# A Mamba2 mixer and feed-forward layer on one core: ACT's gaps moved ahead of the drains, one addition a step later, an earlier root in the last unit, and the prologue's stores issued by SP

## The reference

```
proj = x @ in_proj_w.T                      # 1024 tokens x 512 -> gate, hBC, dt
hBC  = silu(causal_conv4(hBC) + conv_b)     # -> hs (128 heads x 64), B, C (8 groups x 128)
dt   = clip(softplus(dt + dt_bias), 0, 100)
A_cum = cumsum(dt * -exp(A_log)) in chunks of 128 tokens
Y_diag = (C B^T * L) (hs * dt)              # L[l,s] = exp(A_cum[l] - A_cum[s]), s <= l
Y_off  = C . state . exp(A_cum)             # state carried from chunk to chunk
y = (Y_diag + Y_off + hs * D) * silu(gate)
out = rmsnorm_per_group(y) * norm_w @ out_proj_w.T
x = layernorm(x + out);  x = layernorm(x + x @ W.T + bias + lora(x))
```

## Time and profile before

| what | value |
|---|---|
| median of 3 runs | 1631.5 us (1628.75 to 1632.23) |
| the profiled execution | 1630.76 us, its span 1628.9 us |
| mean granted TensorE clock | 0.996 of full speed |
| busy: PE, DVE, ACT, POOL | 1585.0, 1356.4, 1222.4, 1234.6 us |
| DMA | 178.69 MB, mean 110 GB/s |

### The profile page before, as it was taken

One profiled execution on the slowest core, in us unless ns is written; L12 is line 12 of the kernel. 1 busy time (PEld: TensorE's weight loads), 2 busy tenths in 40 slices (PEclk: granted clock), 3 DMA queues, 4 the chain that ended last, 5 costly groups with the idle time before them and its releaser, 6 DMA issues. The chain is left out here.

```text
span 1628.9 us, 27350 instructions
## 1 busy us (share of the span) xinstructions
PE 1585.0 (97%) x9104; PEld 1300.6 (80%) x9104; DVE 1356.4 (83%) x1877; ACT 1222.4 (75%) x2363; POOL 1234.6 (76%) x1019
## 2 busy tenths in 40 slices
PE   8899999999999999999999999999999999999987
PEld 6778888878888788878888788887888788887764
DVE  6577898879979798797988889887997879888786
ACT  5878778777778877886887777887687877778742
POOL 4478778687796868778787878868779696877883
PEclk9999999999999999999999999999999999999999
DMA  3543325233242432433243332423324233343311
GB/s 114 199 166 98 120 79 156 82 111 108 91 151 79 121 98 98 128 97 121 86 119 122 93 121 83 155 79 114 110 85 159 72 121 97 98 138 92 130 53 46
DMA packets 87148, 178.69 MB, mean 110 GB/s; under 512 B 16480, under 2 KB 20576, under 8 KB 86624
## 3 DMA queue, kind: packets, MB, share of 16 engines
q1 hardware_dynamic: 83760, 175.72, 34.0%
q10 hardware_dynamic: 3248, 1.22, 0.3%
HBM read 172.17 MB, written 4.72 MB: 109 GB/s over the span
## 5 line engine op out<-in xcount | busy, mean ns | idle before, releaser
L505 PE MATMUL proj<-x_hi,w_hi 128*128 128x512 f32 x1160 | 462.2, 398 | 11.2 <-DVE x_lo L1274 6.9
L506 PE MATMUL proj<-x_lo,w_hi 128*128 128x512 f32 x1160 | 453.4, 391 | 0.0
L507 PE MATMUL proj<-x_hi,w_lo 128*128 128x512 f32 x1160 | 453.1, 391 | 0.0
L996 POOL TENSOR_TENSOR w_lo<-raw,w_hi 128x512 fp32r<-128x512 f32 x209 | 284.9, 1366 | 110.8 <-ACT w_hi L732 108.1
L1149 DVE SCALAR_TENSOR_TENSOR hs<-proj,uch,hs 128x511 f32<-128x511 f32 (+2 forms) x384 | 285.3, 744 | 58.6 <-ACT hs L759 53.8
L813 ACT ACTIVATE decay<-decay,tok 128x128 f32<-128x128 f32 x1024 | 312.4, 390 | 0.0
L505 PEld LDWEIGHTS proj<-x_hi,w_hi 128*128 128x128 f32 x1160 | 219.0, 189 | 56.5 <-issue 10.5
L1054 POOL TENSOR_TENSOR dh<-dh,eac 128x512 f32<-128x512 f32 x96 | 128.7, 1340 | 169.7 <-DVE eac L1209 169.7
L507 PEld LDWEIGHTS proj<-x_hi,w_lo 128*128 128x128 f32 x1160 | 218.7, 189 | 46.3
L506 PEld LDWEIGHTS proj<-x_lo,w_hi 128*128 128x128 f32 x1160 | 219.1, 189 | 41.9
L1178 DVE TENSOR_TENSOR decay<-decay,cb 128x1024 f32<-128x1024 f32 x128 | 200.2, 1564 | 54.4 <-ACT decay L831 52.0
(11 more groups left out here) (129 smaller groups left out, 3031.4 us busy)
## 6 DMA issues: line engine op xcount, KB each, us to landing
decay<-acum_d SPq DMA_DIRECT2D x128, 512.0 KB, 4.2
raw<-w_t SPq DMA_DIRECT2D x209, 256.0 KB, 2.9
eac<-eacum_d SPq DMA_DIRECT2D x192, 128.0 KB, 3.0
wo_raw<-wo_t SPq DMA_DIRECT2D x32, 256.0 KB, 4.2
c_new<-wo_t SPq DMA_DIRECT2D x32, 256.0 KB, 3.7
hs<-x_t SPq DMA_DIRECT2D x8, 256.0 KB, 5.8
acc<-x_tok SPq DMA_DIRECT2D x1, 2048.0 KB, 8.9
out<-acc SPq DMA_DIRECT2D x8, 256.0 KB, 2.0
```

The lines of the kernel that those rows point to most:

```text
L505: nc.tensor.matmul(dst[:], w_hi[:, ws, k, :], x_hi[:, k, cols], start=(k == 0), stop=False)
L506: nc.tensor.matmul(dst[:], w_hi[:, ws, k, :], x_lo[:, k, cols], start=False, stop=False)
L507: mm = nc.tensor.matmul(dst[:], w_lo[:, ws, k, :], x_hi[:, k, cols], start=False, stop=(k == KC - 1))
L996: nc.gpsimd.tensor_tensor(w_lo[:, s].rearrange("p a b -> p (a b)"), raw[:, s, :], w_hi[:, s].rearrange("p a b -> p (a b)").bitcast(F32), A ...
```

## The change

Nothing is computed differently; instructions change their place in an engine's order, and four stores their engine.

- ACT, loop: in all steps but (g,e,1) (there only (0,0,1) changes), the gaps come ahead of the drain of a one-batch tile, and between the two drains of a two-batch tile. `lookahead` stays behind the last drain, so it comes behind the gaps.
- VectorE: at e = 0 the `add_normed` of chunk 5 moves from step 5 to step 6, which then has two. In the last unit `scale_off` of step 2 comes sooner, and in step 7 `ln_begin(0, 5)` stands directly behind `add_normed`.
- GpSimd, last unit: `rstd_of(0, .)` moves to the next step, behind the state's decay; where a step has no tiles, `decay_hidden` goes ahead of `skip`; in step 7 the root `rs` goes ahead of the gate.
- Prologue: SP issues the four stores, waits for their inputs itself, and issues the first load of `eac` there instead of in the loop. ACT drains H0 to H2 sooner, and takes the first exponential after the first batch's Silus.

```diff
-            wait(q, dh_ready, step(g, e, c))
+            wait(q, dh_ready, 0 if step(g, e, c) == 1 else step(g, e, c))
@@ SP, prologue
+            sp.wait_ge(scanned, 2)
+            sp.dma_start(acum_d.rearrange("c h l -> h c l"), sc[2].rearrange("h (c l) -> h c l", c=CHUNKS)).then_inc(acum_stored, 16)
+            sp.wait_ge(act_pre, 7)
+            for h2 in range(2):
+                sp.dma_start(eacum_d[:, h2].rearrange("c a l -> a c l"),
+                             sc[3][h2:HEADS:2].rearrange("a (c l) -> a c l", c=CHUNKS)).then_inc(eacum_stored, 16)
+            sp.dma_start(elast_d, elc[:]).then_inc(eacum_stored, 16)
             sp.wait_ge(acum_stored, 16)
             load_decay(sp, 0, 0, 0)
...
             sp.wait_ge(eacum_stored, 48)
+            load_eac(sp, 0, 0, 1)
@@ ACT, loop
-                        if tiles:
+                        o2, e2, c2 = ahead(e, c, 2)
+                        o3, e3, c3 = ahead(e, c, 3)
+                        if c == 1 and (g, e) != (0, 0):
                             drain_proj(g, tiles[0])
                             lookahead(g, e, c, 0, last)
-                        if c == 1 and (g, e) != (0, 0):
                             wo_split_hi(g, e, (2, 3))
...
+                            gaps(g + o3, e3, c3)
+                        else:
+                            if tiles and len(tiles[0].batches) == 2:
+                                drain_proj(g, tiles[0], (0,))
+                            if c % 2 == 0:
+                                gaps(g, e, c + 1)
+                            elif not (last and o3):
                                 gaps(g + o3, e3, c3)
-                        else:
-                            gaps(g, e, c + 1)
+                            if tiles:
+                                drain_proj(g, tiles[0], (1,) if len(tiles[0].batches) == 2 else (0,))
+                                lookahead(g, e, c, 0, last)
@@ GpSimd, loop
+                        if last and e == 1 and c >= 3:
+                            rstd_of(0, c - 3)
...
                         if not tiles:
+                            if c == 7:
+                                lagged_rms(g, e, c)
                             gate_y(g, e, c)
-                            lagged_rms(g, e, c)
+                            if c < 7:
+                                lagged_rms(g, e, c)
                             if not (last and off):
+                                decay_hidden(g + off, ne, ncn)
                                 skip(g + off, ne, ncn)
-                                decay_hidden(g + off, ne, ncn)
-                        if last and e == 1 and c >= 2:
-                            rstd_of(0, c - 2)
@@ VectorE, loop
-                        elif e == 0 and c >= 5 and not (g == 0):
+                        elif e == 0 and c >= 6 and not (g == 0):
+                            if c == 6:
+                                add_normed(g - 1, 5)
                             add_normed(g - 1, c)
...
+                        if ffn_step and c == 7:
+                            ln_begin(0, 5)
+                            lns = lns[1:]
```

More of the change, by code:

```diff
@@ L459, in body @@
                         o1, e1, c1 = ahead(e, c, 1)
-                        if c1 % CPB and not (last and o1):
+                        if c1 % CPB and not (last and o1) and (g, e, c) != (0, 0, 0):
                             load_eac(sp, g + o1, e1, c1)
@@ L875, in _ @@
             silus(None, [PROLOGUE[3]])
-            drain_proj(None, PROLOGUE[5], (0,))
+            drain_proj(None, PROLOGUE[5])
             act.wait_ge(scanned, 2)
-            act.dma_start(acum_d.rearrange("c h l -> h c l"), sc[2].rearrange("h (c l) -> h c l", c=CHUNKS)).then_inc(acum_stored, 16)
             v = sc[4].rearrange("p (c l) -> p c l", c=CHUNKS)
@@ L884, in _ @@
             ins.then_inc(act_pre, 1)
-            drain_proj(None, PROLOGUE[5], (1,))
+            drain_proj(None, PROLOGUE[6], (0,))
             nc.scalar.activation(elc[:], a[:, :, P - 1:P].rearrange("p c o -> p (c o)"), ACT.Exp).then_inc(act_pre, 1)
             nc.scalar.activation(sc[3], sc[2], ACT.Exp).then_inc(act_pre, 1)
[L888 to L893, removed]
+            drain_proj(None, PROLOGUE[6], (1,))
             lay_tokens(1, 0)
-            drain_proj(None, PROLOGUE[6], (1,))
-            drain_proj(None, PROLOGUE[7], (0,))
+            drain_proj(None, PROLOGUE[7])
             lay_tokens(2, 2)
@@ L904, in _ @@
             gaps(0, 0, 0)
-            drain_proj(None, PROLOGUE[7], (1,))
+            drain_proj(None, PROLOGUE[8], (0,))
+            silus(None, PROLOGUE[5:9], (0,))
+            drain_proj(None, PROLOGUE[8], (1,))
+            drain_proj(None, PROLOGUE[9])
             act.wait_ge(gap_ready, 1)
             exps(0)
[L908 to L912, removed]
             silus(None, PROLOGUE[5:9], (1,))
@@ L1120, in _ @@
             groups(body)
+            rstd_of(0, 5)
             inv_rms(G, 6)
@@ L1355, in body @@
                             add_normed(g, c - 2)
-                        elif e == 0 and c >= 5 and not (g == 0):
+                        elif e == 0 and c >= 6 and not (g == 0):
+                            if c == 6:
+                                add_normed(g - 1, 5)
                             add_normed(g - 1, c)
                         lns = [(w, c - (2, 5)[w]) for w in range(2) if ffn_step and c >= (2, 5)[w]]
-                        if ffn_step and c in (1, 4, 5, 6):
+                        if ffn_step and c in (1, 2, 4, 5, 6):
                             scale_off(g, e, c + 1)
+                        if ffn_step and c == 7:
+                            ln_begin(0, 5)
+                            lns = lns[1:]
                         for ln in lns:
@@ L1401, in body @@
                             low_gated(s)
-                        if ffn_step and c in (0, 2):
+                        if ffn_step and c == 0:
                             scale_off(g, e, c + 1)
```

## The result

The changed kernel takes 1637.45 us (median of 10 runs, 1633.1 to 1641.16) against 1629.67 for the kernel before in the same rounds: ratio 1.0044, 95% interval 1.0033 to 1.0056. It is 0.44% slower, some 7 us; the forecast was 1621 and the range ended at 1628. The profiled execution took 1635.34 us, its span 1633.5.

A forecast was written before the change was run, and what follows sets the result against it. TensorE, busy 1585.0 of 1628.9 us, was taken as the bound, leaving 44 us of idling to win. Terms -7.7 + 1.4 - 2.0 - 1.8 = -10.1 us gave 1621 us; 8-in-10 range 1612 to 1628.

The forecast's parts named there:

- (g,0,6), predicted 7 x 1.1 = 7.7 us: Step 6 at e = 0, groups 1 to 7: moving the addition removes TensorE's wait for `eac`, winning 7.7 us.
- Gaps ahead elsewhere, +0.2 a group, +1.4, ends -6.3 and +6.3: Other loop steps: gaps ahead of drains delay `w_hi` and GpSimd, costing 0.2 us a group, +1.4 in all.
- makes this wait 0.2 to 0.4 longer: TensorE's 0.94 us `p_out` wait at (g,0,1): GpSimd 1.3 us late lengthens it by 0.2 to 0.4 us.
- 1.07 us at (g,1,3): Step 3 at e = 1: time to spare between `xd_lo` ending and TensorE taking it, 1.07 us.
- I price it at nothing: VectorE's two additions in step 6 at e = 0 cost nothing; without cover, at most 1.7 us.
- Rival (A): Loop: the split behind the gaps makes `xd_lo` or `w_lo` TensorE's last wait; +16 us, 1647 us; chance 0.08.
- Prologue, predicted -2.0: Program start: earlier `eac` load and drains win 2.0 us; ends -4.5 and +1.0.
- the 1.6 us for the lower clock behind 48.17: Prologue: the late tile H2 ran at granted clock 0.63, costing 1.6 us that earlier drains would remove.
- Last unit, predicted -1.8: Program end: earlier root `rs` and reordering shorten TensorE's 2.66 us wait at 1602.24, winning 1.8 us; ends 0 and -3.5.
- its far end: Last unit's best case, -3.5 us: the wait gone and the lower clock behind it too.

The follow-up runs named there:

- e1: Kernel before with only the addition of chunk 5 moved from step (g,0,5) to (g,0,6): 1620.38 us, ratio 0.9946.
- e11: Changed kernel with ACT's split ahead of the gaps in one-batch steps and VectorE's third `wo_lo` ahead of the state addition at c = 1: 1606.84 us, ratio 0.9855.
- e5: Changed kernel with ACT's loop order as in the kernel before (gaps behind drains and split): 1614.21 us, ratio 0.9898.
- e3: Kernel before with the prologue's edits alone: 1628.18 us, ratio 0.9986.
- e2: Kernel before with ACT's loop order alone changed (gaps ahead of the drains): 1644.05 us, ratio 1.0082.
- e4: Kernel before with the last unit's VectorE and GpSimd edits alone: 1626.01 us, ratio 0.9978.
- e10: Changed kernel with VectorE's split of the last two output weights (`wo_lo` 2 and 3) moved later, behind `front`: 1639.38 us, ratio 1.0052 to the kernel before.
- e12: e11 with ACT's split (`lookahead`) ahead of the second drain in two-batch steps: 1603.90 us, ratio 0.9841 to the kernel before.

## Why the prediction was wrong

1. **(g,0,6), predicted 7 x 1.1 = 7.7 us: right in kind, too small.** The wait went in all seven groups; e1 measured 0.54%, 8.8 us, and the traces 1.45 us each, 10.2 in all. The idle entry was 1.22, but consecutive matmuls overlap by 0.24 in the records, and a wait costs that too: 1.22 + 0.24 = 1.46. The same sum holds for the new waits (0.73 + 0.24 against a lag of 1.00) and for e11 (0.47 + 0.24 against 0.75).
2. **"Gaps ahead elsewhere, +0.2 a group, +1.4, ends -6.3 and +6.3": the step that failed.** This term priced the late split. The step-by-step comparison of the changed kernel with e5 gives 1.21 + 1.00 + 0.55 - 0.23 = +2.5 a group, 17.7 us in seven groups, beyond the upper end. Two things were wrong in it.
   - At (g,0,1) I wrote that a GpSimd 1.3 us late "makes this wait 0.2 to 0.4 longer". `dh`, for which VectorE's `y` waits, ends at 469.66 + 1.74 = 471.40, 1.41 us later than before (469.99), while TensorE was 0.93 us ahead by that time: 2.34 us late against TensorE. VectorE's slack took up a part, and the wait grew by 1.21: 0.93 because the last two `wo_lo` start at the same time as before while TensorE is ahead, 0.28 because they take longer. The gate did get its 1 us back, 1.29 instead of 2.27, as predicted. But `w_lo` was 1.41 late and `dh` is still 1.41 late: the 1 us was paid by the instructions behind, above all by `rs` (1.54 instead of 0.54), which now runs beside VectorE's mix of 461.32 to 463.10, 2 us sooner than before, and by `dh` itself (1.74 instead of 1.29). That is what the Trainium skill's "SBUF — State Buffer", "Who interferes with whom", says, which I had weighed and set aside: the later one of the two blocks. Here the trace agrees with it.
   - (g,1,0) is not in the prediction. Its margin, 1.57 us, is in none of its rows; it took 1.07 us at (g,1,3) for the tightest and stood it in for the rest. That one was not touched: in two-batch steps ACT arrives early enough, as predicted, and no wait came. Nor did the prediction price the `proj` wait for `w_lo` at (g,1,1).
3. **"I price it at nothing": the addition in step 6.** True for VectorE, as e1 shows; but the gain itself has a price. TensorE arrives 1.45 us sooner at (g,1,0) and spends the margin on which the gaps edit rested. I priced the edits apart and added them. Rival (A) had the mechanism: its places (g,1,7) and (g,0,7), "about 1 each", are the ones that cost, those at (g,1,3) and (g,0,5) gave no wait; I gave it 0.08 because I let ACT's earlier arrival pay for it everywhere, and in the one-batch steps there is no idle time between drains from which it could.
4. **Prologue, predicted -2.0:** right, e3 -2.3 us (0.14%), with the wait near 75 (4.48 in e3, 4.09 in the changed kernel) and the clock behind it at 0.59 in both. One piece of its sum does not hold: the 1.6 us for the lower clock behind 48.17 is not a fixed cost. In e1, e2 and e4, whose prologue is that of before, the clock there was 1.00, and TensorE waited for the next tile instead (1.30 us at 51.94 in e1). And the loop order takes 1.0 us back in the first steps: `p_yd` at (0,0,2) is 2.8 us sooner in e3, 1.75 in the changed kernel, which waits 0.77 us at 86.56 for a `w_lo`.
5. **Last unit, predicted -1.8:** right in kind, half the size; e4 measured 0.22%, 3.6 us. The end wait went from 2.66 to 0.99 as forecast. The rest is the 1.6 us of lower clock that vanished behind it, which the prediction had only in its far end.

The parts alone are -8.8 (e1), +13.4 (e2), -2.3 (e3) and -3.6 (e4), together -1.3 us; the lags that only addition and gaps together give are 7 x (1.00 + 0.34) = 9.4 us. That makes +8.1 against the +7.2 measured; four ratios, uncertain by 0.1% each, are in the sum.

## What to carry to other kernels

List for every place where two engines meet the margin by which the second-last arrives ahead of the last, not only the places that wait. An edit that delays a producer and an edit that lets the consumer come sooner both spend it, so they can't be priced apart. An operation that feeds a chain on another engine (here a 0.6 us split) goes ahead of a long block for which the engine that bounds the kernel does not wait: that order turned +0.44% into -1.22%.

## What the runs showed of the hardware

Behind a wait of TensorE of 1.9 us or more the granted clock sometimes fell to the lower of its two levels (1.2 instead of 2.4 GHz), and not at the same place from one trace to the next. In the 14 traces, 7 of the 26 `p_out` waits of 1.9 us or more were followed by a dozen matmuls at 0.34 us and more apiece instead of 0.23, against 1 of 74 waits between 0.3 and 1.9 us. Windows behind two nearly equal waits (2.13 and 1.96 us) of the changed kernel: stretch, us, PE, PEld, DVE, ACT, POOL busy, PEclk, DMA share, GB/s:

```profile
1058.46:1061.46 3.00, 3.00 (x14) 2.51 (x15) 2.90 (x6) 1.02 (x3) 3.00 (x3) 1.00 0.92 333
1252.60:1255.60 3.00, 3.00 (x8) 2.32 (x9) 2.90 (x6) 1.02 (x3) 3.00 (x3) 0.53 0.98 349
```

The second cost 1.6 us. The ten runs of the changed kernel fall in order of their mean clock: 1633.1 us at 0.997, 1635.3 to 1636.0 at 0.995, 1639 to 1641 at 0.993. So such a wait costs more than itself on average. At two places the fall came more regularly: behind the prologue's wait near 75 the clock was at 0.50 to 0.61 in all nine traces in which that wait is 3.5 to 4.5 us, and at 1.00 in e10, where it is 3.1; and it fell behind the wait of 2.65 us near the end in all four traces that have it (the kernel before, e1, e2, e3). Length is not all: behind the 6.9 us wait at the very start no trace shows a fall. One more such place is in the last unit, behind waits of 0.9 and 1.8 us, with a fall in 4 of the 10 traces that have the pair. The window there in e11:

```profile
1537.30:1545.16 7.86, 6.08 (x9) 2.67 (x10) 7.25 (x13) 5.59 (x12) 6.33 (x6) 0.63 0.09 33
```

The same stretch in e12:

```profile
1536.19:1544.05 7.86, 6.08 (x25) 3.65 (x26) 7.42 (x14) 5.63 (x13) 6.33 (x6) 1.00 0.10 33
```

Both windows begin with the same state product; in the same time e12 gets through 25 matmuls and e11 through 9, with the clock at 1.00 and at 0.63, and 3.0 us lie between them by the end of that step. Whether a wait of 3.5 us in the loop makes the clock fall each time stays open, since e10 did not make one.
